# An LSTM recurrence on one core: half 0's output gate ahead of half 1's cell gates, and x sums in the body's first three steps

## The reference

```python
def step(carry, xw_t):                      # xw_t = x_t @ Wx + b
    prev_h, prev_c = carry
    a = xw_t + prev_h @ Wh
    i, f, o = sigmoid(a[:, :H]), sigmoid(a[:, H:2*H]), sigmoid(a[:, 2*H:3*H])
    g = tanh(a[:, 3*H:])
    next_c = f * prev_c + i * g
    next_h = o * tanh(next_c)
    return (next_h, next_c), next_h
x = x + lstm(x)                             # 1024 steps, one after the other
ys = cond / sqrt(256)
x = x + (x * ys[:, None, :]) @ w * rsqrt((ys * ys) @ (w * w) + 1e-8)[:, None, :]
```

## Time and profile before

| | us |
|---|---|
| median of 3 runs | 1954.5 |
| lowest, highest | 1953.48, 1954.77 |
| the profiled execution | 1955.69 |
| its span, first to last instruction | 1953.9 |
| TensorE busy in the span | 1861.5 |
| DVE busy | 918.0 |
| ACT busy | 900.8 |
| POOL busy | 251.2 |

### The profile page before, as it was taken

One profiled execution on the slowest core, in us unless ns is written; L12 is line 12 of the kernel. 1 busy time (PEld: TensorE's weight loads), 2 busy tenths in 40 slices (PEclk: granted clock), 3 DMA queues, 4 the chain that ended last, 5 costly groups with the idle time before them and its releaser, 6 DMA issues.

```text
span 1953.9 us, 360822 instructions
## 1 busy us (share of the span) xinstructions
PE 1861.5 (95%) x166792; PEld 1742.5 (89%) x166792; DVE 918.0 (47%) x11034; ACT 900.8 (46%) x6148; POOL 251.2 (13%) x1295
## 2 busy tenths in 40 slices
PE   7999999999999999999999999999999999999998
PEld 6988899898989989898998989899898989989896
DVE  2444444444444444444444444444444444444444
ACT  1444444444444444444444444444444444444443
POOL 0111111111111111111111111111111111111110
PEclk7999999999999999999999999999999999999999
DMA  2000000000000000000000000000000000000001
GB/s 65 29 0 0 0 0 0 0 0 0 0 0 0 0 0 0 0 0 0 0 0 0 0 0 0 0 0 0 0 0 0 0 0 0 0 0 0 0 0 43
DMA packets 4586, 6.71 MB, mean 3 GB/s; under 512 B 1248, under 2 KB 3040, under 8 KB 4576
## 3 DMA queue, kind: packets, MB, share of 16 engines
q1 hardware_dynamic: 3872, 5.51, 0.9%
q10 hardware_dynamic: 704, 1.05, 0.1%
HBM read 4.46 MB, written 2.10 MB: 3 GB/s over the span
## 4 chain that ended last, share of the span: by engine, by line
PE 82%; DVE 10%; ACT 5%; issue 3%; DVEq 0%
PE pG L214 46%; PE pX L196 18%; PE pF L227 9%; PE pS L214 8%; DVE junk L353 6%; ACT gates L181 5%; DVE hst L364 2%; DVE pG L334 1%; PE pX L302 1%; DVE gates L353 0%; PE pS L293 0%; DVE ores L381 0%; PE pG L223 0%; PE pS L223 0%; ACT ogate L185 0%
## 5 line engine op out<-in xcount | busy, mean ns | idle before, releaser
L214 PE MATMUL pG<-hst,wh_sb 128*32 128x16 f32 x98304 | 1137.8, 186 | 56.0 <-DVE hst L364 53.2
L214 PEld LDWEIGHTS pG<-hst,wh_sb 128*32 128x32 f32 x98304 | 1039.3, 111 | 140.4 <-DVE hst L364 121.4
L353 DVE CUSTOM_DVE_ANT_1 junk<-gates 128x4 f32<-128x4 f32 x4096 | 507.6, 162 | 908.6 <-ACT gates L181 856.3
L181 ACT ACTIVATE gates<-pG 128x6 f32<-128x6 f32 x2048 | 371.4, 181 | 1016.7 <-PE pG L214 870.3
L214 PE MATMUL pS<-hst,wh_sb 128*32 128x16 f32 x32768 | 495.9, 185 | 2.8 <-issue 2.8
L227 PE MATMUL pF<-zeros,picks 128*32 128x128 f32 x2624 | 471.0, 280 | 0.0
L196 PE MATMUL pX<-xp,wx_sb 128*32 128x8 f32 x33024 | 443.7, 180 | 28.3 <-issue 5.0
L196 PEld LDWEIGHTS pX<-xp,wx_sb 128*32 128x32 f32 x33024 | 375.2, 109 | 53.5 <-DVE pG L334 47.7
L187 ACT ACTIVATE tanhc<-gates 128x2 f32<-128x2 f32 x2048 | 410.4, 200 | 12.9
L214 PEld LDWEIGHTS pS<-hst,wh_sb 128*32 128x32 f32 x32768 | 398.2, 108 | 3.0 <-issue 3.0
L364 DVE TENSOR_TENSOR hst<-tanhc,ogate 128x2 f32<-128x2 f32 x2048 | 330.5, 161 | 103.3 <-ACT tanhc L187 3.3
(11 more groups left out here) (31 smaller groups left out, 14.0 us busy)
## 6 DMA issues: line engine op xcount, KB each, us to landing
outT_dram<-ores SPq DMA_DIRECT2D x8, 256.0 KB, 2.5
xh<-in_xT_dram SPq DMA_DIRECT2D x6, 320.0 KB
wh_sb<-in_Wh_dram ACTq DMA_DIRECT2D x1, 1024.0 KB, 7.7
wx_sb<-in_Wx_dram SPq DMA_DIRECT2D x1, 1024.0 KB, 7.3
w_sb<-in_w_dram SPq DMA_DIRECT2D x1, 256.0 KB, 6.4
xh<-in_xT_dram SPq DMA_DIRECT2D x2, 64.0 KB, 7.7
condT<-in_condT_dram ACTq DMA_DIRECT2D x1, 2.0 KB, 7.5
bias_col<-in_bC_dram ACTq DMA_DIRECT2D x1, 3.0 KB, 7.2
```

Source lines behind the costliest of these rows:

```text
L181: act.activation(gates[:, j, :, 0:NG].rearrange("p b n -> p n b"), cells[j][:, :, cols], ACT.Sigmoid).then_inc(gates_ready[j], 1)
L214: last = pe.matmul(to[c * Q:(c + 1) * Q, :], tile(wh_sb[:, k, :], c, j, g), hst[:, k, WIDE * t:WIDE * (t + 1)], start=False, stop=True, sk ...
L353: cell = dve.tensor_tensor_reduce(out=junk[:, j, b, :], in0=gates[:, j, b, AT_I:AT_F + 1].unsqueeze(2).broadcast_to([P, 2, 2]), in1=gates[ ...
```

## The change

LEAD goes: step s works on time slot s, so the carries fall into the body's last step and the x sums, for the next body, into its first three. Only one group of x sums is made before the loop. Half 0's out products stand ahead of half 1's cell products: their first k before the wait for h of half 1, behind a wait for `x_carried[K]` (the out carry) in the body's first step, and their second k right behind `sums_ready[0]`. ACT runs `ogate` 0 between `gates` 0 and `gates` 1. The waits for `xh_ready` inside the body are dropped, and POOL's spread stands behind the fourth add. WARM is 26 instead of 32, and FILL is (0, 0, 1, 1) instead of (1, 1, 2, 1). The offsets LEAD in the addresses of `xh` are dropped too, with the memset of its first columns; those lines are left out here, and so are the renamed slots.

```diff
-    LEAD = T - 1
-    WARM = 32
-    FILL = (1, 1, 2, 1)
+    WARM = 26
+    FILL = (0, 0, 1, 1)
...
             def bodies(lo, hi, aside=None):
...
-                        if s == T - 1:
-                            pool.wait_ge(x_summed, it + 3)
-                            spread(bass.ds(it * T + 3 * T, T))
-                        now = xh[:, :, :, bass.ds(it * T + (LEAD + s), 1)]
-                        pool.tensor_tensor(now, now, hst[:, :, h_slot(s):h_slot(s) + B].unsqueeze(3), ALU.add).then_inc(xh_ready, 1)
+                        at = h_slot((s + 1) % T)
+                        now = xh[:, :, :, bass.ds(it * T + s, 1)]
+                        pool.tensor_tensor(now, now, hst[:, :, at:at + B].unsqueeze(3), ALU.add).then_inc(xh_ready, 1)
+                    pool.wait_ge(x_summed, it + 2)
+                    spread(bass.ds(it * T + 2 * T, T))
...
-                    for j in range(K):
+                    def cell_gates(j):
                         act.wait_ge(sums_ready[j], it * T + (s + 1))
                         act.activation(gates[:, j, :, 0:NG].rearrange("p b n -> p n b"), cells[j][:, :, cols],
                                        ACT.Sigmoid).then_inc(gates_ready[j], 1)
-                    for j in range(K):
+
+                    def out_gate(j):
                         act.wait_ge(osum_ready[j], it * T + (s + 1))
                         act.activation(ogate[:, j, :], outs[j][:, cols], ACT.Sigmoid)
+
+                    def cell_tanh(j):
                         act.wait_ge(cell_ready[j], it * T + (s + 1))
                         act.activation(tanhc[:, j, :], gates[:, j, :, AT_C], ACT.Tanh, scale=2.0).then_inc(tanh_ready[j], 1)
+
+                    cell_gates(0)
+                    out_gate(0)
+                    cell_gates(1)
+                    cell_tanh(0)
+                    out_gate(1)
+                    cell_tanh(1)
...
-            for n in range(2):
-                pe.wait_ge(xp_ready, n + 1)
-                for j in range(K):
-                    if n:
-                        pe.wait_ge(x_carried[j], n)
-                    sum_x_cells(j)
-                if n:
-                    pe.wait_ge(x_carried[K], n)
-                sum_x_outs().then_inc(x_summed, 1)
+            pe.wait_ge(xp_ready, 1)
+            for j in range(K):
+                sum_x_cells(j)
+            sum_x_outs().then_inc(x_summed, 1)
             pe.wait_ge(operands_ready, 3)
+            pe.wait_ge(x_carried[0], 1)
 
             early, late = range(G // 2), range(G // 2, G)
             with pe.Fori(0, NBODY) as it:
                 for s in range(T):
-                    t = (s + LEAD) % T
                     pe.wait_ge(h_ready[0], it * T + (s + 1))
                     for n in range(NG):
-                        cell(t, 0, n, 0)
-                    if t == 0:
-                        pe.wait_ge(x_carried[1], it + 2)
-                    cell(t, 1, 0, 0)
-                    cell(t, 1, 1, 0, early)
+                        cell(s, 0, n, 0)
+                    if s == 0:
+                        pe.wait_ge(x_carried[K], it + 1)
+                    add_h(outs[0], s, 0, O_, 0)
+                    cell(s, 1, 0, 0)
+                    cell(s, 1, 1, 0, early)
 
                     pe.wait_ge(h_ready[1], it * T + (s + 1))
                     for n in range(NG):
-                        last = cell(t, 0, n, 1)
+                        last = cell(s, 0, n, 1)
                     last.then_inc(sums_ready[0], 1)
-                    cell(t, 1, 1, 0, late)
-                    cell(t, 1, 2, 0)
+                    add_h(outs[0], s, 0, O_, 1).then_inc(osum_ready[0], 1)
+                    cell(s, 1, 1, 0, late)
+                    cell(s, 1, 2, 0)
                     for n in range(NG):
-                        last = cell(t, 1, n, 1)
+                        last = cell(s, 1, n, 1)
                     last.then_inc(sums_ready[1], 1)
-                    if t == 0:
-                        pe.wait_ge(x_carried[K], it + 2)
-                    for j in range(K):
-                        add_h(outs[j], t, j, O_, 0)
-                        add_h(outs[j], t, j, O_, 1).then_inc(osum_ready[j], 1)
+                    for k in range(K):
+                        last = add_h(outs[1], s, 1, O_, k)
+                    last.then_inc(osum_ready[1], 1)
 
                     if s == 0:
-                        pe.wait_ge(xp_ready, it + 3)
-                        pe.wait_ge(x_carried[0], it + 2)
+                        pe.wait_ge(xp_ready, it + 2)
                         sum_x_cells(0)
                     elif s == 1:
-                        pe.wait_ge(xh_ready, it * T + T)
                         sum_x_cells(1)
                     elif s == 2:
                         sum_x_outs().then_inc(x_summed, 1)
...
-                        if t == T - 1 and j == 0:
+                        if s == T - 1 and j == 0:
                             carry_cells(0)
...
-                        if t == T - 1 and j == 0:
+                        if s == T - 1 and j == 0:
                             carry_cells(1)
-                    if t == T - 1:
+                    if s == T - 1:
                         carry_outs()
```

More of the change, by code:

```diff
@@ L44, in build @@
         picks = sb("picks", [P, Q])
-        xh = sb("xh", [P, K, B, SEQ + 3 * T])
+        xh = sb("xh", [P, K, B, SEQ + 2 * T])
         xp = sb("xp", [P, K, ROWS])
@@ L83, in build @@
         gates_ready = [sem(f"gates_ready{j}") for j in range(K)]
-        x_edged, bias_doubled = sem("x_edged"), sem("bias_doubled")
+        bias_doubled = sem("bias_doubled")
         x_carried = [sem(f"x_carried{n}") for n in range(K + 1)]
@@ L105, in _ @@
             for k in range(K):
-                sp.dma_start(xh[:, k, :, LEAD:LEAD + XCUT[1]], xT_in[k * P:(k + 1) * P, :, 0:XCUT[1]]).then_inc(x_begun, 16)
+                sp.dma_start(xh[:, k, :, 0:XCUT[1]], xT_in[k * P:(k + 1) * P, :, 0:XCUT[1]]).then_inc(x_begun, 16)
             sp.wait_ge(h_ready[0], 2 * T)
@@ L109, in _ @@
                 for k in range(K):
-                    sp.dma_start(xh[:, k, :, LEAD + lo:LEAD + hi], xT_in[k * P:(k + 1) * P, :, lo:hi]).then_inc(x_loaded, 16)
+                    sp.dma_start(xh[:, k, :, lo:hi], xT_in[k * P:(k + 1) * P, :, lo:hi]).then_inc(x_loaded, 16)
             sp.dma_start(w_sb[:, :, :], w.rearrange("(k p) o -> p k o", p=P)).then_inc(w_loaded, 16)
@@ L120, in _ @@
         def _(pool):
-            pool.memset(xh[:, :, :, 0:LEAD], 0.0).then_inc(x_edged, 1)
-            pool.memset(xh[:, :, :, LEAD + SEQ:SEQ + 3 * T], 0.0).then_inc(xh_ready, T)
+            pool.memset(xh[:, :, :, SEQ:SEQ + 2 * T], 0.0).then_inc(xh_ready, T)
             def spread(t):
                 pool.tensor_copy(xp[:, :, :].rearrange("p k (t b) -> p k b t", b=B), xh[:, :, :, t]).then_inc(xp_ready, 1)
-            pool.wait_ge(x_edged, 1)
             pool.wait_ge(x_begun, 16 * K)
             spread(slice(0, T))
-            for n in range(1, 3):
-                pool.wait_ge(x_summed, n)
-                spread(slice(n * T, (n + 1) * T))
+            pool.wait_ge(x_summed, 1)
+            spread(slice(T, 2 * T))
             def bodies(lo, hi, aside=None):
@@ L176, in _ @@
                 for s in range(T):
-                    t = (s + LEAD) % T
-                    cols = slice(B * t, B * (t + 1))
-                    for j in range(K):
+                    cols = slice(B * s, B * (s + 1))
+                    def cell_gates(j):
                         act.wait_ge(sums_ready[j], it * T + (s + 1))
@@ L302, in _ @@
                     last = pe.matmul(pO[n % 2][:, :], wmod[:, b, k, o * P:(o + 1) * P],
-                                     xh[:, k, b, LEAD + ch * NOUT:LEAD + (ch + 1) * NOUT], start=(k == 0), stop=(k == K - 1))
+                                     xh[:, k, b, ch * NOUT:(ch + 1) * NOUT], start=(k == 0), stop=(k == K - 1))
                 last.then_inc(layer_summed, 1)
@@ L330, in _ @@
             for j in range(K):
-                dve.tensor_copy(hst[:, j, h_slot(LEAD):h_slot(LEAD) + B], condT[:, j, :]).then_inc(h_ready[j], 1)
+                dve.tensor_copy(hst[:, j, h_slot(0):h_slot(0) + B], condT[:, j, :]).then_inc(h_ready[j], 1)
             def carry_cells(j):
@@ L362, in _ @@
                         dve.wait_ge(tanh_ready[j], it * T + (s + 1))
-                        at = h_slot((t + 1) % T)
+                        at = h_slot((s + 1) % T)
                         dve.tensor_tensor(hst[:, j, at:at + B], tanhc[:, j, :], ogate[:, j, :], ALU.mult).then_inc(h_ready[j], 1)
-                        if t == T - 1 and j == 0:
+                        if s == T - 1 and j == 0:
                             carry_cells(1)
-                    if t == T - 1:
+                    if s == T - 1:
                         carry_outs()
@@ L381, in _ @@
                 dve.scalar_tensor_tensor(out=ores[:, n % 2, :], in0=pO[n % 2][:, :], scalar=demod[:, o, b:b + 1],
```

(2 more changed lines are left out.)

1 line of the change is left out of this document (removed).

## The result

| | before | after |
|---|---|---|
| median, us | 1953.99 | 2007.15 |
| lowest, highest | 1952.52, 1954.77 | 2006.49, 2007.77 |
| span of the profiled execution | 1953.9 | 2006.0 |
| mean granted clock | 0.994 | 0.995 |

After is slower: the ratio is 1.0273, with an interval of 1.0255 to 1.0291. The forecast was 2045 us in a range of 1972 to 2080. The sign and the range held; of the 91 us forecast, 53 came.

The account below looks back on a forecast made before the run. The prediction took the chain from one h to the next, through gates 1 and half 1's cells, as the bound: 7.43 - 0.35 + 0.56 + 0.16 = 7.80 us a body; 1954.5 + 95 - 4.2 = 2045 us, range 1972 to 2080.

Parts of the forecast that it names:

- overrun of x sums and fillers gone: TensorE's x sums and fillers outlasting the wait for the next h would no longer delay steps: -0.35 us a body.
- part 2: On ACT, half 0's out gate sigmoid ahead of gates 1 gains nothing, hst 0 standing behind half 1's cells: 0.
- Rival C: TensorE's stream is the bound, so fewer fillers make the kernel faster: 1847 us, chance 9%.
- Part 1: On TensorE, 16 out products moved ahead of gates 1 lengthen each step by 0.14 us: +0.56 us a body.
- Rival E: TensorE waits for half 1's h, so the 8 products moved ahead of it are free: 1973 us, chance 4%.
- Part 4: In the body's first step TensorE waits for the out carry, which DVE makes last: +0.16 us a body.
- Rival B: The out carry wait costs nothing because DVE finishes that carry earlier: 2004 us, chance 8%.
- Part 3: Behind gates 1, x sums and fillers fit TensorE's 0.81 us of room before the next h: -0.35 us a body.
- Part 6: Before the loop, one block of 128 x products and 12 warm-up records go: -4.2 us, once.
- Rival D: TensorE's granted clock falls to 1.2 GHz in the loop: near 2630 us if it lasted, chance 6%.

Follow-up runs that it names:

- e1: Changed kernel with the old order within a step put back on TensorE and ACT, out carry wait included; 1865.8 us, ratio 0.9548.
- e3: Changed kernel with the out carry split by half, half 0's ahead of hst 1 on DVE, each half awaited separately; 1947.1 us, ratio 0.9966.
- e4: Kernel before with one edit, FILL (0, 0, 1, 1) instead of (1, 1, 2, 1); 1880.1 us, ratio 0.9619.
- e10: Changed kernel without TensorE's signal behind half 0's out products, ACT running that out gate behind gates 1; 1980.8 us, ratio 1.0126.
- e5: Changed kernel with half 0's out sum signalled late, behind 14 products of half 1's out gate, and ACT's order put back; 2026.8 us, ratio 1.0372.
- e9: Kernel of e1 with tanh 0 ahead of half 0's out gate sigmoid on ACT; 1881.4 us, ratio 0.9624 against the kernel before.
- e2: Changed kernel with only ACT's order put back (gates 0, gates 1, out gate 0, tanh 0); 2007.4 us, ratio 1.0274.
- e6: Changed kernel with the old FILL (1, 1, 2, 1); 2014.8 us, ratio 1.0310.
- e8: Kernel of e1 without fillers, FILL (0, 0, 0, 0); 1863.6 us, ratio 0.9535 against the kernel before.

## Why the prediction was right in sign and too high in size

Step by step, in the terms of the sum, a body:

| term | predicted | measured | from |
|---|---|---|---|
| overrun of x sums and fillers gone | -0.35 | -0.35 (-0.32 in e1) | four steps of 1.77 against 7.43; e1 has 7.11 a body on average |
| 16 products ahead of gates 1, four steps | +0.56 | +0.63 | start to gates 1 1.255 against 1.097 on average, of it 0.026 a step for the signal |
| out gate's sigmoid early | 0 | -0.28 | gates 1 to hst 0 0.39 against 0.46, four steps |
| wait for the out carry | +0.16 | +0.25 | first step 2.11, the others 1.85; e3 gives 60 us (0.23) back |
| start, once | -4.2 us | -6.4 us | ninth h0 |

**What bounds the kernel** was read rightly in that it is the chain from one h to the next, and not TensorE's total work, with x sums and fillers in its shadow or not. The end of that chain was read wrongly: in the kernel before it ran over half 0's out products, their sigmoid and tanh 0 to hst 0, and not over gates 1 and half 1's cells (part 2 below). In the changed kernel it does run over the cells. Rival C, that TensorE's stream is the bound and less filler work makes the kernel faster, failed in the form in which it was priced. It is worth a second look, though: fewer fillers alone do make the kernel before 3.8% faster (e4), not because TensorE is the bound, but because two steps of four overran. That was the 0.35 of the prediction, and e1 and e4 confirm it.

**Part 1** (the products move ahead) held: 0.14 forecast, 0.16 found, the rest being one more signal ahead of gates 1 that the sum didn't have. e1 and e10 show both. Rival E fell: TensorE did not stand at the wait for h1, or the 8 products ahead of it would have been free, and gates 0 came 0.84 after the start instead of 0.77.

**Part 2 is the step that failed.** I wrote that the early sigmoid "gains nothing", since hst 0 stood behind half 1's cells on DVE. The prediction named this as a sign of being wrong: hst 0 earlier than 0.46 after gates 1. It came 0.39 after. The rows had two candidates for the release of hst 0 at 1005.79: the tanh, done at 1005.75, and the cells. I took the cells, because they came directly ahead. The cells' last record overlaps hst 0: the changed kernel starts hst 0 (1005.36) together with the last accumulator read (1005.36). So the cells would have let it go at 0.39, and it was the tanh, queued on ACT behind the out gate's sigmoid that waited for its sum, that held it to 0.46. e5 shows this: with the out sum signalled late, hst 0 is at 0.44 again, and in e9, where the sigmoid comes last, it follows the sigmoid. What gains is that the sum is there early, and not the place on ACT (e2). The page's after-side hint is the wait of DVE's hst for tanhc, 132.1 us in 665 waits, which is hst 1 alone, three steps a body.

**Part 4 was mis-sized for the same reason.** hst 0 came 0.07 earlier and hst 1 did not (0.36 behind it instead of 0.29), so the out carry behind hst 1 lies 0.07 later against h0. What is left, some 0.02, no run isolates; e3, where the wait is gone, still has 1.87 instead of 1.85 in that step, so it need not be the wait's. The gain of part 2 is thus real in three steps of a body and given back in the fourth. Rival B's 2004 us lies close to the measured 2007, but its mechanism did not happen: the wait is there and costs 60 us. A right number from a wrong mechanism is worth nothing here.

**The sum** with the measured sizes, 7.43 - 0.35 + 0.63 - 0.28 + 0.25, is 7.68, against 7.67 measured over the same 200 bodies. The rest is rounding and 0.02 that no term has: on average the first product follows the start of hst 0 by 0.211 instead of 0.216, in four steps. The forecast came as near as it did because its errors partly cancelled: part 2 was 0.28 a body too high (72 us), parts 1 and 4 together 0.16 too low (41 us).

**Part 3**, on the fillers' cover, held: e6 shows 8 us for six records more. **Part 6**, the start, was short by 2.2 us. The block was right in size (the first hst starts at 15.56 instead of 19.79, 4.2 us), but the half clock ended sooner as well. Before (stretch, busy times, granted clock):

```profile
34.00:38.00 4.00, 2.75 (x164) 2.31 (x162) 0.84 (x10) 0.89 (x6) 0.34 (x2) 0.50 0.00 0
38.00:42.00 4.00, 4.00 (x306) 3.94 (x298) 1.75 (x22) 1.65 (x12) 0.23 (x2) 0.62 0.00 0
```

and after:

```profile
30.00:34.00 4.00, 3.94 (x267) 3.44 (x261) 1.79 (x23) 1.74 (x12) 0.39 (x2) 0.53 0.00 0
34.00:38.00 4.00, 3.92 (x393) 3.56 (x384) 1.49 (x20) 1.64 (x12) 0.45 (x3) 1.00 0.00 0
```

The granted clock goes from 1.2 back to 2.4 GHz near the end of 30 to 34 us (mean 0.53, then 1.00) instead of within 38 to 42 (mean 0.62). Rival D, the fall of the clock in the loop, did not come.

## What to carry to other kernels

Where two engines' work ends within a few hundredths of a microsecond ahead of the instruction that you ask about, the row before it need not be its release: price the edit under both, since an early signal may free one while the other has already let go. When an order is changed on the engine that all others follow, count what now stands ahead of the last signal of the chain, products and signals alike, and look at the carries and waits that a later instruction of the same engine now sits behind. And undo a mixed change in parts: here the fillers, the shift and the shorter start were worth 88 us, while the reorder that went with them cost 141.

## What the runs showed of the hardware

- A completion signal of TensorE between two groups of products cost 0.026 us of its stream, in each of 1024 steps (e10).
- On DVE the 128x2 multiply started together with the last accumulator read of the instruction before, 0.08 us ahead of that read's end (changed kernel, 1005.36).
- On ACT a sigmoid followed a tanh by 0.11 us (e9), a tanh a sigmoid by 0.05 (e2) to 0.07 (e1).
- A wait with 0.165 us of idle in the records lengthened its step by 0.25 us, and taking it away gave 0.23 back (e3).
- With no filler at all and TensorE waiting for h in two steps of a body, the granted clock stayed at 2.4 GHz (e8). That kernel, at 1863.6 us, 4.65% below the kernel before, has the lowest median here; e1, with two fillers a body, is at 1865.8, and the two intervals overlap.
